# A two-layer adaLN / RWKV / mixture-of-experts kernel, rebuilt: rows stored indirectly into expert slots, first attention off GpSimd, values spread by broadcast loads

## The reference

```python
def block(x, mod, attention, experts):          # run twice, with different attentions
    sa, ca, ga, sb, cb, gb = mod                 # from silu(c) @ wmod, per batch; |ga|, |gb| >= 0.25
    x = x + ga * attention(layernorm(x) * (1 + ca) + sa)
    x = x + gb * experts(layernorm(x) * (1 + cb) + sb)
    return x

# layer 0 attention (RWKV-4): r, v, k = x @ W_rvk.T ; over time, per channel, with w = -exp(time_decay):
#   p = max(pp, u + k); y = (e^(pp-p) aa + e^(u+k-p) v) / (e^(pp-p) bb + e^(u+k-p))
#   pp' = max(pp + w, k); aa, bb decay and add likewise;  out = (sigmoid(r) * y) @ W_out.T
# layer 1 attention (RWKV-6): five mixes of x and its predecessor through tanh and small matrices,
#   r, k, v, gate g, decay d; 16 heads of 8 channels, an 8x8 state each:
#   y = r . (S + u k v^T) ; S' = d S + k v^T ; then a norm per head, times silu(g), times Wo
# experts (both layers): router = softmax(x @ Wr), the best 2 of 8 experts, weights normalised to 1,
#   out = sum over the two of weight * (act(x @ W1[e] + b1[e]) @ W2[e] + b2[e]), 128 -> 512 -> 128
#   (gelu with biases in layer 0, silu without in layer 1)
```

## Time and profile before

| | |
|---|---|
| Time, median of 3 runs | 672.38 us |
| Runs | 666.99, 672.38, 674.42 us |
| Span of the profiled execution | 673.3 us (the trace gives no other time for it) |
| Granted TensorE clock, mean | 0.838 of full |
| Busy: PE / DVE / POOL / ACT | 514.8 / 330.1 / 256.1 / 203.3 us |
| Moved by DMA | 70.27 MB, 104 GB/s on average |

### The profile page before, as it was taken

How to read it: one execution, slowest core, us unless ns; L and a number is a source line. 1 busy time by engine, 2 the same in 40 slices (tenths; PEclk the granted TensorE clock), 3 DMA queues, 4 the chain that set the end, 5 groups by cost and what they waited for, 6 DMA issues and landing times. The chain is left out here.

```text
span 673.3 us, 7874 instructions
## 1 busy us (share of the span) xinstructions
PE 514.8 (76%) x2600; PEld 371.7 (55%) x2600; DVE 330.1 (49%) x624; ACT 203.3 (30%) x457; POOL 256.1 (38%) x238
## 2 busy tenths in 40 slices
PE   6952444787988789997788679997788996777763
PEld 5420224476977677346355544534454986767663
DVE  2799997533600015435986687534777546100000
ACT  2042510325535335345122013025111443033330
POOL 1062600762465643102644000306975223646440
PEclk9785665696998899976999777568989998689897
DMA  7000005255564655203100201402342543757623
GB/s 234 0 0 1 0 28 190 52 133 145 178 203 136 220 200 154 65 28 88 47 8 2 62 0 57 182 12 67 84 100 82 173 143 85 242 161 216 185 86 125
DMA packets 28744, 70.27 MB, mean 104 GB/s; under 512 B 5938, under 2 KB 10662, under 8 KB 28704
## 3 DMA queue, kind: packets, MB, share of 16 engines
q1 hardware_dynamic: 18656, 57.43, 27.1%
q0 software_dynamic: 5888, 10.25, 6.2%
q10 hardware_dynamic: 4160, 2.10, 1.1%
HBM read 62.40 MB, written 9.18 MB: 106 GB/s over the span
## 5 line engine op out<-in xcount | busy, mean ns | idle before, releaser
L437 POOL DMA_INDIRECT y_rows<-ys,dest x92 | 98.1, 1067 | 171.2 <-ACT ys L600 156.0
L430 POOL DMA_INDIRECT xg<-h_rows,source x92 | 93.0, 1010 | 152.2 <-DVE source L1266 108.3
L839 PE MATMUL PP<-w_ring,hid 128*128 128x128 f32 x736 | 109.3, 296 | 29.9 <-ACT hid L587 15.0
L839 PEld LDWEIGHTS PP<-w_ring,hid 128*128 128x128 f32 x736 | 95.4, 201 | 44.5 <-issue 22.9
L824 PE MATMUL PP<-xs,w_ring 128*128 128x128 f32 x736 | 100.3, 289 | 1.5 <-ACT xs L574 0.8
L824 PEld LDWEIGHTS PP<-xs,w_ring 128*128 128x128 f32 x736 | 96.3, 206 | 6.6 <-issue 5.7
L1275 DVE SCALAR_TENSOR_TENSOR x<-PP,gate,x 128x512 f32<-128x512 f32 x8 | 6.0, 750 | 163.6 <-PE PP L885 94.9
L600 ACT ACTIVATE ys<-PP,slot_gate 128x128 f32<-128x128 f32 x92 | 33.8, 370 | 128.7 <-PE PP L839 101.3
L587 ACT ACTIVATE hid<-PP,b1q 128x128 f32<-128x128 f32 x184 | 51.9, 379 | 52.1 <-PE PP L824 36.1
L463 POOL TENSOR_TENSOR arena<-arena 128x512 f32<-128x512 f32 x32 | 38.0, 1189 | 21.7 <-DVE arena L1322 19.4
L945 PE MATMUL PP<-arena,consts 128*128 128x512 f32 x64 | 35.5, 637 | 11.0 <-POOL arena L463 10.7
(11 more groups left out here) (193 smaller groups left out, 747.7 us busy)
## 6 DMA issues: line engine op xcount, KB each, us to landing
w_ring<-experts_dram SPq DMA_DIRECT2D x92, 512.0 KB
h_rows<-htok ACTq DMA_DIRECT2D x4, 512.0 KB
xg<-h_rows,source POOLq DMA_INDIRECT x92
y_rows<-ys,dest POOLq DMA_INDIRECT x92
x<-x_t_dram SPq DMA_DIRECT2D x4, 256.0 KB, 5.9
out_t_dram<-x SPq DMA_DIRECT2D x4, 256.0 KB, 3.7
H<-wmod_dram SPq DMA_DIRECT2D x1, 768.0 KB, 6.7
consts<-consts_dram SPq DMA_DIRECT2D x1, 704.0 KB, 7.5
```

The lines of the kernel that those rows point to most:

```text
L430: pool.indirect_dma_start(xg[:, n % XG, :], None, h_rows[h], bass.IndirectOffsetOnAxis(source[:, h % 2, q:q + 1], 0)).then_inc(s_xg[n % XG ...
L437: pool.indirect_dma_start(y_rows[h], bass.IndirectOffsetOnAxis(dest[:, h % 2, q:q + 1], 0), ys[:, n % YR, :], None, bounds_check=TOPK * T ...
L839: last = pe.matmul(ps, hid[:, n % HID, c * P:(c + 1) * P], w_ring[:, n % WR, FH + c * P:FH + (c + 1) * P], start=(c == 0 and h >= NB), sto ...
```

## The change

The diff touches almost every stage. In words:

- **Groups.** Experts are run for five groups and no longer four halves: layer 0 of either batch, layer 1 of batch 0, and the two blocks of 512 tokens of layer 1 of batch 1 each by themselves. Blocks of 128 slots: 23, 23, 23, 15 and 15, 99 in all. The ring of weights holds 5.
- **Slots.** No inversion. The slot of a (token, expert) is known to the token, so POOL stores the normalised rows of 128 tokens at a time indirectly into `xg_rows` (two stores for 128 tokens), which SP has filled with zeros at the start; SP loads slots with plain loads, four blocks at a time. Results are stored plainly by SP, in slot order and without weights. When a group is stored, POOL gathers for each 128 tokens their two rows, and PE adds them against diagonal matrices that hold the two weights; in layer 0 the second bias is added there. The router's softmax is replaced by a tanh of half the difference of the two best logits.
- **First attention.** Everything is written with D = k - running maximum: the exponents are clamped (ScalarE Relu), the two others become sigmoids; POOL takes no part, DVE reads k from PSUM, the quotient goes by the logarithm in both batches.
- **Normalisation.** The matrix is identity minus 1/128, so its product is centred already; ScalarE squares and copies it; the inverse root is spread by small products of a broadcast column with the identity. The norm over a head likewise.
- **Second attention.** v is stored to DRAM; for each j SP loads it back spread over the head's partitions by a broadcast source. Batch 0 runs 8 steps of 1024 tokens, batch 1 8 steps for each of its two blocks. POOL's product with r goes to DVE. Decay and gate are taken by ScalarE straight from PSUM. When the first block of batch 1 has its states, its tail (group norm, norm, route, experts) runs beside the second block's states.
- **Order.** New strings, one also for SP.

The core of the diff:

```diff
-NQ = (TOPK * T + NE * (P - 1)) // P
-XG, WR, YR, HID = 8, 6, 4, 2
+GROUPS = ((0, 0, (0, 1)), (0, 1, (0, 1)), (1, 0, (0, 1)), (1, 1, (0,)), (1, 1, (1,)))
+GT = [TPB * len(g[2]) for g in GROUPS]
+NQ = [(TOPK * P * t + NE * (P - 1)) // P for t in GT]
+UNIT = 4
+WR, XG, HID, YR, VS = 5, 3, 2, 6, 3
...
     "POOL":
-        "a4 b4 g15 s2 g5 s g s g2 s6 g s g3 s g s2 g3 s g s2 g2 s g2 s g s2 g3 s g s2 g2 s g s g s2 g s11 a4 "
...
+        "p32 g32 p24 g2 p8 g30",
...
+            sp.wait_ge(s_set, 10)
+            for g in range(NG):
+                sp.dma_start(xg_rows[g].rearrange("(p r) n -> p (r n)", p=P), zeros[:, 0:NQ[g] * P]).then_inc(s_zeroed, 16)
...
+            def spreads():
...
+                            sp.dma_start(vs[m % VS][:, 0:width],
+                                         heads[j][:, at0:at0 + width].unsqueeze(1).broadcast_to([P // HK, HK, width])).then_inc(s_vs[m % VS], 16)
...
+            def puts():
...
+                            pool.indirect_dma_start(xg_rows[g], bass.IndirectOffsetOnAxis(row_of[:, g, k, t:t + 1], 0),
+                                                    htok[:, t, :], None, bounds_check=NQ[g] * P - 1,
+                                                    oob_is_err=False).then_inc(s_put, 16)
+            def gets():
...
+                                for p in range(YR):
+                                    pool.wait_ge(s_yst[p], 16 * ((Q0[g + 1] - 1 - p) // YR + 1))
...
+                            pool.indirect_dma_start(yt[:, k, t, :], None, y_rows[g],
+                                                    bass.IndirectOffsetOnAxis(row_of[:, g, k, t:t + 1], 0)).then_inc(s_got[t // TPB], 16)
...
+            def attn0(b):                                    # ScalarE
+                act.activation(A["E1"], A["D"], ACT.Relu, bias=wpos).then_inc(s_rel[b], 1)
+                act.activation(A["E2"], A["D"], ACT.Relu, bias=wneg, scale=-1.0).then_inc(s_rel[b], 1)
+                act.activation(A["E1"], A["E1"], ACT.Exp, scale=-1.0).then_inc(s_e[b], 1)
+                act.activation(A["E2"], A["E2"], ACT.Exp, scale=-1.0).then_inc(s_e[b], 1)
+                act.activation(A["Sn"], A["D"], ACT.Sigmoid, bias=uneg, scale=-1.0).then_inc(s_sg[b], 1)
+                act.activation(A["S"], A["D"], ACT.Sigmoid, bias=u).then_inc(s_sg[b], 1)
...
+            def attn0_sums(b):                               # VectorE
+                link(dve.tensor_tensor_scan(A["bb"][:, 1:T + 1], A["E1"], A["E2"], 0.0, ALU.mult, ALU.add))
+                link(dve.tensor_tensor(A["pp"][:, 0:T], A["E2"], A["V"], ALU.mult))
+                dve.scalar_tensor_tensor(A["D"], A["bb"][:, 0:T], -1.0, A["Sn"], ALU.add, ALU.mult).then_inc(s_den[b], 1)
+                link(dve.tensor_tensor_scan(A["aa"][:, 1:T + 1], A["E1"], A["pp"][:, 0:T], 0.0, ALU.mult, ALU.add))
+                link(dve.tensor_tensor(A["Sn"], A["Sn"], A["aa"][:, 0:T], ALU.mult))
+                link(dve.tensor_tensor(A["S"], A["S"], A["V"], ALU.mult))
+                link(dve.tensor_tensor(A["Sn"], A["Sn"], A["S"], ALU.add))
...
+            def attn1_state(b, part):                        # VectorE, per j
+                    dve.wait_ge(s_vs[m % VS], 16 * (m // VS + 1))
+                    dve.tensor_tensor(kv[:, 0:width], A["K"][:, span], vs[m % VS][:, 0:width], ALU.mult).then_inc(s_kv[b], 1)
+                    link(dve.tensor_tensor_scan(S[:, 1:width + 1], A["dec"][:, span], kv[:, 0:width], start, ALU.mult, ALU.add))
+                    link_prod(b, j, n, part, dve.tensor_tensor(prod[n % 2][:, 0:width], A["R"][:, span], S[:, 0:width], ALU.mult))
...
+            def tail(i):
+                yield from group_norm(1, (i,))
+                yield from layer_norm(3, 1, (i,))
+                yield from route(3 + i)
+                yield from finish(3 + i)
```

More of the change, by code:

```diff
@@ L107, in merged, with job @@
         run(parts)
[L110 to L124, removed]
+def job(name):
+    return [n for n, _ in JOBS].index(name)
 def program(nc, x_d, wrvk_d, wout0_d, cols_d, wmod_d, wp_d, b1_d, b2_d, br_d, wr_d,
             maaw1_d, maaw2_d, tdw1_d, tdw2_d, wproj_d, const_d, out_d, gate_d):
-    h_rows = [nc.dram_tensor(f"h_rows{h}", (T, P), F32, kind="Internal").ap() for h in range(HALVES)]
-    y_rows = [nc.dram_tensor(f"y_rows{h}", (TOPK * T, P), F32, kind="Internal").ap() for h in range(HALVES)]
+    xg_rows = [nc.dram_tensor(f"xg_rows{g}", (NQ[g] * P, P), F32, kind="Internal").ap() for g in range(NG)]
+    y_rows = [nc.dram_tensor(f"y_rows{g}", (NQ[g] * P, P), F32, kind="Internal").ap() for g in range(NG)]
+    v_rows = [nc.dram_tensor(f"v_rows{b}", (P, T), F32, kind="Internal").ap() for b in range(NB)]
     with ExitStack() as ctx:
@@ L405, in _, with results @@
+            def results():
+                for b in range(NB):
+                    for i in range(BPB):
+                        yield
+                        sp.wait_ge(s_xup[b][i], 4)
+                        sp.dma_start(blk(out_d, BPB * b + i), x_blk(b, i)).then_inc(s_done, 16)
+            merged(ORDER.get("SP", ""), w=weights(), l=slots(), y=rows(), v=spreads(), o=results())
             sp.wait_ge(s_done, 16 * NBLK)
@@ L496, in _ @@
+            merged(ORDER.get("POOL", ""), p=puts(), g=gets())
         @block.scalar
@@ new lines, in second @@
+            def second():
+                yield from layer_norm(0, 1, (0, 1))
+                yield from attn0(1)
+                yield from layer_norm(1, 1, (0, 1))
+                yield from route(1)
+                yield from layer_norm(2, 1, (0, 1))
+                yield from attn1_proj(1)
+            def tail(i):
+                yield from group_norm(1, (i,))
+                yield from layer_norm(3, 1, (i,))
+                yield from route(3 + i)
+            merged(ORDER.get("ACT", ""), a=first(), b=second(), c=tail(0), d=tail(1), t=turned(), h=hidden(), w=copied())
@@ new lines, in attn1_sums @@
+            def attn1_sums(b, part):
+                for j in range(HK):
+                    n = step(b, part[0], j)
+                    yield
+                    pe.wait_ge(s_prod[b], n + 1)
+                    if j == 0:
+                        pe.wait_ge(s_y0[b], BPB)
+                    for k, i in enumerate(part):
+                        last = pe.matmul(sums(b, i), headsum[:, j, :], blk(prod[n % 2], k), start=(j == 0), stop=(j == HK - 1),
+                                         skip_group_check=True)
+                    last.then_inc(s_yps[b], 1)
@@ new lines, in second @@
+            def second():
+                yield from layer_norm(0, 1, (0, 1))
+                yield from attn0(1)
+                yield from attn0_out(1)
+                yield from layer_norm(1, 1, (0, 1))
+                yield from route(1)
+                yield from finish(1)
+                yield from layer_norm(2, 1, (0, 1))
+                yield from attn1_proj(1)
+                yield from attn1_bonus(1)
+                yield from attn1_sums(1, (0,))
+                yield from attn1_sums(1, (1,))
@@ L1011, in _, with tail @@
+            def tail(i):
+                yield from group_norm(1, (i,))
+                yield from layer_norm(3, 1, (i,))
+                yield from route(3 + i)
+                yield from finish(3 + i)
+            merged(ORDER.get("PE", ""), m=modulation(), a=first(), b=second(), c=tail(0), d=tail(1), t=turned(), f=all_first(), s=all_second())
         @block.vector
@@ L1424, with tail @@
+            def tail(i):
+                yield from group_norm(1, (i,))
+                yield from layer_norm(3, 1, (i,))
+                yield from route(3 + i)
+                yield from finish(3 + i)
+            merged(ORDER.get("DVE", ""), m=modulation(), k=constants(), a=first(), b=second(), c=tail(0), d=tail(1))
 def kernel(**inputs):
```

1684 lines of the change are left out of this document (815 added, 869 removed), and 29 rows, old and new, of the table ORDER.

## The result

The changed kernel took **629.62 us** (median of four runs, 619.22 to 634.06) beside 670.29 for the kernel before in the same comparison: ratio 0.936, 95% interval 0.922 to 0.950. The forecast was 550, range 510 to 610. The sign was right and a third of the gain came.

The account below looks back on a forecast made before the run. POOL's in-order queue was taken to hold the expert stream, and DVE, slowed by POOL, the attentions. Gains of 13, 37, 10, 22, 14 and 27 us took the 673.3 span to 550, range 510 to 610.

Parts of the forecast that it names:

- The step that failed: First expert group: with plain block stores and loads on SP, a block takes 2.6 us, bounds 2.3 and 3.1.
- First attention, slots, first product: Start to first expert product: quotient at about 53, slots known at 81, products from 112 instead of 124.6, gain 13.
- First group: Layer 0, batch 0 experts: 23 blocks at 2.6 us from 112, ending at 172.
- One add at 199: First group's results, gathered back and summed, are added to x at 199, against 248.7.
- Projections of batch 0, 46 us: Between first add and state loop 0: 56.3 us falls to 46, by decay and gate passes and normalisation, so 245.
- State loops: Second attention: batch 0 eight steps of 4.73 us, 38; batch 1 sixteen half steps, 46.
- Last stage: From 367: throughput of 53 blocks ends at 527, dependence chain at 529; the end adds 21, giving 550.
- Transfers bind: Rival: DMA engines bind, so expert blocks stay at 3.1 us; 606 us in all, chance 15%.
- Indirect transfers wait for scans: Rival: beside DVE work each indirect transfer waits a whole scan, 2.29 us added to 1.0; 601 us, chance 8%.
- PE alone binds: Rival: blocks at PE's 2.3 us, norms fully covered, waits in groups gone; 517 us, chance 8%.
- Broadcast loads hold the steps: Slower rival: spread-value loads queue on SP; 5.1 us more per state step is even, 7 gives 718; chance 4%.
- The rule weighed: Skill's rule for state loop: DVE and GpSimd share a locked port pair, the later blocks a whole instruction, lengthening the sum.

Follow-up runs that it names:

- e3: Changed kernel plus 16 extra plain transfers (1 MB) on GpSimd's queue behind the first group's stores: 578.15 us, ratio 0.895 to the kernel before.
- e9: Changed kernel with all 128 indirect transfers made plain ones of the same bytes, rows unsorted: 556.20 us, ratio 0.828 to the kernel before.
- e6: Changed kernel with three order edits (batch 1's rank products earlier, slot loads before weights, group 0's second sum behind its first): 640.25 us, ratio 0.942.
- e4: Changed kernel with batch 1's rank products moved in PE's order from behind block 17 to behind block 0: 576.92 us, ratio 0.895.
- e8: Changed kernel with weight loads behind the first five bringing only the first matrix, 24 MB less: 631.25 us, ratio 0.931.
- e7: Changed kernel without the broadcast loads of spread values behind the first three, stale values used: 620.71 us, ratio 0.916.
- e14: Changed kernel plus 16 extra indirect gathers with rows of 16 bytes behind group 0's stores: 641.14 us, ratio 0.954.
- e11: Changed kernel plus 16 extra indirect gathers with rows of 512 bytes behind group 0's stores: 650.26 us, ratio 0.967.
- e12: Changed kernel plus 16 extra plain transfers of 64 KB behind group 0's stores, in the third comparison: 634.16 us, ratio 0.944.
- e13: Changed kernel plus 20 GpSimd products of 128 x 512 numbers and no extra transfer, behind group 0's stores: 627.88 us, ratio 0.935.
- e5: Changed kernel unaltered, run again in the second comparison: 634.99 us, ratio 0.937 to the kernel before at 678.68.

## Why the forecast was wrong, and where it was right

**The step that failed** is "block stores and loads are plain transfers on SP, so I take 2.6 us" a block, and 2.3 in the last stage: the indirect transfers that remained were priced for themselves (1.0 to 1.8 us each) and as free for the expert blocks beside them. What the runs show in its place is that PE stands still beside them: a block of group 0 takes 2.9 us with the holds and 2.3 without, the last stage 195 us instead of the 162 of the forecast, and the whole some 57 us more (578 to 635).

The holds are not the whole miss. Without them the same marks (e3) end at 571.3, 21 us over the forecast: 13 of them are there at state loop 0 and all 21 at batch 1's adds, from the second add and the projections (below). That 550 lies only 1.1% under e9, the kernel without indirect transfers, is luck: the forecast had paid for 16 indirect stores with 24 us and for 16 gathers with 29, which are cheaper in e9, and was short elsewhere.

The trace of before had the sign of it. I read the windows of the earlier trace rows as GpSimd's two issues a block, since the quickest stretch is the one with fewest of them. But I did not weigh the waits without a releaser. Beside two of DVE (64.8 and 11.0 us, once each) that trace has these of ScalarE (the list of waits: us in total, times, longest):

```profile
ACT ys L600 <- remote: 24.6, 6, 6.1
ACT hid L587 <- remote: 16.0, 5, 6.7
...
ACT hid L591 <- remote: 8.7, 3, 4.6
```

49 us on the expert blocks, at most (a part of such a wait can be an ordinary one); the changed kernel has 47 in the same three groups:

```profile
ACT hid L630 <- remote: 19.2, 4, 12.4
ACT hid L626 <- remote: 18.6, 3, 9.6
ACT ys L638 <- remote: 9.0, 2, 5.4
```

Fewer transfers, 128 against 184, and as much hold: they come in unbroken rows of 8 to 24 beside dense products, where before each pair waited for its block. From the comparison without holds to those with them, the kernel before takes 26 to 34 us more, the changed one 57 (578 to 635). That is why the ratio is 0.937 with them and 0.895 without; without indirect transfers on either side it is 556 to 610, 0.91.

**Point by point**, against the marks of this trace and of e3, which has no holds:

| mark | forecast | this trace | e3 |
|---|---|---|---|
| first product | 112 | 114.7 | 111.0 |
| group 0's last block | 172 | 180.3 | 164.3 |
| its adds to x | 199 | 209.3, 224.6 | 190.6, 204.3 |
| state loop 0, first scan | 245 + 1 | 277.7 | 259.1 |
| batch 1's adds | 303 | 325.9, 340.8 | 307.4, 324.0 |
| state loop 1, first scan | 363 + 1 | 406.6 | 386.8 |
| second layer's experts | 367 | 416.0 | 395.7 |
| last block's product | 529 | 610.8 | 549.5 |
| end | 550 | 632.3 | 571.3 |

- *First attention, slots, first product:* right within 3 us. The slots were known at 81.0, as forecast. The 16 stores took 82.1 to 105.4; the first product then had batch 1's norm and logits ahead of it in PE's order.
- *First group:* 53 us without holds (e3) against my 60; 66 with them.
- *One add at 199:* there are two halves, 14 to 15 us apart, and PE's order puts blocks 27 to 29 between them. I forecast the first and built on it.
- *Projections of batch 0, 46 us:* mis-sized. I had summed a chain of waits. In e3 it takes 55 from the second add, and PE is full:

```profile
204.00:278.00 74.00, 71.15 (x372) 46.75 (x371) 46.29 (x61) 40.36 (x108) 0.00 (x0) 0.98 0.55 153
```

  71.15 us busy of 74, with the blocks of group 1 woven in. Moving the second sum up (e6) didn't help for that reason.
- *State loops:* 4.92 us a step against 4.73, and 61 us for the second: right, and so are "group norm waits for batch 1's add" and the 42 us of the next stretch (in e4, 41 from the last pass of the norms at 345.9 to 386.7).
- *Last stage:* 154 us from its first to its last product without holds (e3), against 162; with them 195. The end: 21.5 us against 21.
- *Rivals.* Transfers bind: the share of 0.95 at 125 to 150 looked like it, but PE did 13 blocks there, and half the weight bytes (e8) gave 4 us at most. Indirect transfers wait for scans: those from state loop 0 on (303 to 326) took 1.17 us in the mean and 2.1 at most, not 3. PE alone binds: from 204 to 278 it does. Broadcast loads hold the steps: no (e7). The rival that came true, indirect transfers hold PE, was not on my list. *The rule weighed* spoke of DVE and GpSimd, and of 1.48 against 1.00 us; the cost was at another engine.

## What to carry to other kernels

A wait that no row explains, on an engine that needs only one other engine's result, meant here that this result came late: add such waits up before calling the stretch bound by anything else, and see what runs beside each. Price indirect transfers by what they do to PE beside them, not by their own 1 us; place them where PE has no dense products (beside the state loop and the projections no product was late here, though what those transfers cost was not tested by itself), and replace them with plain ones where the order of rows allows it. And when one kernel's time differs between comparisons by 5 to 10%, compare ratios only beside a kernel before that ran with it: here 0.937 and 0.895 are both true.

## What the runs showed of the hardware that I had not expected

- Beside 16 indirect transfers issued back to back, PE finished 90 or 91 products in 25 us instead of 189 to 213 (e14, e11 against e12, e13, e5 and the first trace), and ScalarE waited up to 12.4 us for products whose end the profile had long before, at a granted clock that fell only afterwards. The Trainium skill, "SBUF — State Buffer", "Who interferes with whom", states that "PE and ACT never wait on anyone". It speaks of the ports of SBUF. ScalarE's passes did keep their durations (0.28 and 1.14 us), as it says; PE was held, and no run here shows whether at a port or elsewhere.
- It comes and goes with something outside the kernels: in four comparisons of five the kernel before took 667 to 682 and the holds were there in each kept trace with indirect transfers beside experts, in one it took 640 to 644 and there were none. Whether that is the chip isn't shown; one with holds and the one without have the same chip number.
- Rows of 16 bytes hold it as rows of 512 do (13 and 16 us for sixteen transfers), and arithmetic on GpSimd, 20 us of it, does not.
- What does it stays open: whether it is the writing of the addresses, the fetching of them, or something between them and PE's report of an end. Every timed run here was recorded with its clock, so none tells whether it exists unrecorded.
